# Large attention layers: exponentials behind the next unit's squares and values, reciprocals and probabilities behind its normalisation

## What is computed

```python
q = (hidden_states @ q_proj_w.T).reshape(B, Q, NUM_HEADS, HEAD_DIM).transpose(0, 2, 1, 3)
k = (cross_attention_states @ k_proj_w.T) ...
v = (cross_attention_states @ v_proj_w.T) ...
q = rmsnorm(q, q_norm_w); k = rmsnorm(k, k_norm_w)
scores = jnp.einsum('bhqd,bhkd->bhqk', q, k) * scale + attention_mask
attn = jax.nn.softmax(scores, axis=-1)
out = jnp.einsum('bhqk,bhkd->bhqd', attn, v)
x = x + jnp.tanh(g_xattn[1]) * (out @ o_proj_w.T)
```

## Time and profile before

| | |
|---|---|
| median of 3 runs | 3029.27 us (3025.58 to 3031.83) |
| the profiled execution | 3028.03 us |
| its span, first to last instruction | 3026.2 us |
| TensorE busy | 2552.8 us (84%) |
| VectorE busy | 1838.3 us (61%) |
| ScalarE busy | 1314.6 us (43%) |
| GpSimd busy | 1287.3 us (43%) |
| mean granted TensorE clock | 0.938 of full |

### The profile page before, as it was taken

One profiled execution on the slowest core, in us unless ns is written; L12 is line 12 of the kernel. 1 busy time (PEld: TensorE's weight loads), 2 busy tenths in 40 slices (PEclk: granted clock), 3 DMA queues, 4 the chain that ended last, 5 costly groups with the idle time before them and its releaser, 6 DMA issues. The chain is left out here.

```text
span 3026.2 us, 42470 instructions
## 1 busy us (share of the span) xinstructions
PE 2552.8 (84%) x13827; PEld 2149.3 (71%) x13827; DVE 1838.3 (61%) x3455; ACT 1314.6 (43%) x3752; POOL 1287.3 (43%) x1423
## 2 busy tenths in 40 slices
PE   3899999997679999998878886978579999999655
PEld 2788888875568888887757775745468888888544
DVE  3676777766556666666646664522456666666655
ACT  2454444443235555554424443123145555555223
POOL 4444444442124444444326554333334444444235
PEclk9899999998889999999999997989799999999868
DMA  3101111110002222211000001278111111110037
GB/s 105 49 29 36 33 36 36 36 32 25 13 22 83 82 88 91 77 36 53 32 9 10 8 8 55 56 242 291 47 31 45 32 32 36 33 35 5 9 125 262
DMA packets 69103, 178.95 MB, mean 59 GB/s; under 512 B 10516, under 2 KB 11218, under 8 KB 66683
## 3 DMA queue, kind: packets, MB, share of 16 engines
q1 hardware_dynamic: 52048, 112.25, 11.5%
q0 software_dynamic: 13632, 61.10, 6.1%
q10 hardware_dynamic: 3210, 2.89, 0.3%
HBM read 157.84 MB, written 37.25 MB: 64 GB/s over the span
## 5 line engine op out<-in xcount | busy, mean ns | idle before, releaser
L1991 POOL TENSOR_TENSOR W<-W,rden 128x512 f32<-128x512 f32 x192 | 199.9, 1041 | 839.3 <-DVE rden L1460 839.3
L1167 ACT ACTIVATE W<-S,nmx 128x128 f32<-128x128 f32 x768 | 299.3, 391 | 514.4 <-DVE nmx L1455 514.4
L1952 POOL TENSOR_TENSOR S<-S,mask 128x512 f32<-128x512 f32 x192 | 248.9, 1296 | 107.9 <-ACT S L1011 107.7
L1011 ACT ACTIVATE oT_h<-B_oT 128x512 fp32r<-128x512 f32 x200 | 119.9, 600 | 286.1 <-PE B_oT L733 281.3
L1460 DVE RECIPROCAL rden<-den 128x4 f32<-128x4 f32 x192 | 34.2, 178 | 327.2 <-ACT W L1167 327.2
L1473 DVE SCALAR_TENSOR_TENSOR X<-B_out,gates,X 128x512 f32<-128x512 f32 x216 | 161.5, 747 | 111.3 <-PE B_out L662 111.0
L662 PE MATMUL B_out<-ring_h,oT_h 128*128 128x512 f32 x516 | 208.9, 405 | 18.1 <-DVE X L1473 8.8
L662 PE MATMUL B_qkv<-ring_h,xnT_h 128*128 128x512 f32 x512 | 217.3, 424 | 5.0 <-DVE xnT_l L1309 5.0
L713 PE MATMUL B_s<-kT,qT_h 128*128 128x256 f32 x768 | 207.9, 348 | 4.1 <-DVE S L1452 2.5
L703 PE MATMUL B_qT<-ident,qk 128*128 128x128 f32 x768 | 130.1, 294 | 94.8 <-DVE qk L1423 68.4
L662 PE MATMUL B_out<-ring_l,oT_h 128*128 128x512 f32 x516 | 207.7, 402 | 0.0
(11 more groups left out here) (446 smaller groups left out, 8044.7 us busy)
## 6 DMA issues: line engine op xcount, KB each, us to landing
raw<-in_pieces SPq DMA_DIRECT2D x270, 256.0 KB, 2.7
slots_y<-S SPq DMA_DIRECT2D x31, 256.0 KB, 4.2
slots_y<-y SPq DMA_DIRECT2D x15, 256.0 KB, 5.5
X<-in_x ACTq DMA_DIRECT2D x8, 256.0 KB, 2.8
raw<-in_ctxT SPq DMA_DIRECT2D x8, 256.0 KB, 2.7
rows_x<-xn SPq DMA_DIRECT2D x8, 256.0 KB, 2.0
out_x<-X SPq DMA_DIRECT2D x8, 256.0 KB, 3.6
raw<-in_quant SPq DMA_DIRECT2D x4, 256.0 KB, 2.6
```

The costliest lines, as they stand in the source:

```text
L1011: return act.activation(dst, src, ACT.Copy, scale=scale)
L1167: t = act.activation(W[:, k, cols(r)], S[:, k, cols(r)], ACT.Exp, bias=nmx[:, k, r:r + 1], accum_out=den[:, k, r:r + 1])
L1952: pool.tensor_tensor(S3, S3, m.unsqueeze(1).to_broadcast([P, R, P]), ALU.add).then_inc(*masked.now((layer, u)))
L1991: pool.tensor_tensor(W3, W3, rden[:, k, :].unsqueeze(2).to_broadcast([P, R, P]), ALU.mult).then_inc(*probs.now((layer, u)))
```

## The change

Two order numbers of `Schedule.attention` change. The exponentials of unit i stay in step i + 2 but go from order 60 to 71, behind `project` of unit i + 2. The event `probs` (VectorE's reciprocal and GpSimd's multiplication) goes from step i + 2, order 65, to step i + 3, order 11, behind `normalise` of unit i + 2 and ahead of `times_v`, `turn_p`, `scores`, and of the `mask` of unit i + 1. The instructions themselves, their number and their semaphores are the same, and so are the programs of TensorE and of the SP queue. The `next` events at 90 (and, outside the middle units, at 5) now come ahead of `probs`.

```diff
@@ -141,8 +141,8 @@
             self.at(i + 2, 40, "scores", layer, u)
             self.at(i + 2, 41, "low_scores", layer, u)
             self.at(i + 2, 56, "mask", layer, u)
-            self.at(i + 2, 60, "exp", layer, u)
-            self.at(i + 2, 65, "probs", layer, u)
+            self.at(i + 2, 71, "exp", layer, u)
+            self.at(i + 3, 11, "probs", layer, u)
             self.at(i + lag - 2, 30, "turn_p", layer, u)
             self.at(i + lag - 1, 20, "times_v", layer, u)
             self.at(i + lag, 0, "attn_out", layer, u, needs=five[3:5],
```

## The result

The changed kernel takes 2917.7 us in the median of four runs (2910.31 to 2920.50), against 3029.31 us (3025.58 to 3031.83) before: a ratio of 0.9629, 95% interval 0.9608 to 0.9650, some 112 us less. Its profiled execution was the fastest of the four: 2910.31 us, span 2908.5 us, mean granted clock 0.940 (0.938 before). The spans differ by 3026.2 - 2908.5 = 117.7 us.

The account below looks back on a forecast made before the run. TensorE, the busiest engine, waits for q and k because exponentials precede the square on ScalarE. From 3028.0 us, minus 68 (steady units) and 23 (looser stretches) gives 2937, plus 1.2 for the median: 2938 us, range 2916 to 2984.

Parts of the forecast that it names:

- layer 0's steady gain: Layer 0's middle 48 units: floor 9.50 us, excess 3.0 us per eight-unit cycle, six cycles, 18 us gained.
- the loss of layer 1's first four units: Where layer 1 begins: exponentials leave idle ScalarE time and delay the low-rank copies, 1 us each, minus 4 us.
- Layer 0's two ends and layer 3's end: Two or three units each with a late maximum, 1.4 to 2 us a unit: 12 us gained, an estimate.
- the floor of layers 1 and 3: TensorE's own period in steady units there, taken as 9.64 us from four consecutive transposes without a wait.
- my 50 us: Steady gain of layers 1 and 3: 25 us each, from 4.2 us excess per cycle, six cycles.
- the looser stretches: Units outside the flat stretches: 23 us gained in sum, bounds 42 us above and minus 10 below.
- layer 3's start: Late maximum, exponentials hold square and VectorE's sums: 1.8 us a step, five steps, 9 us gained.
- Layer 1's end: Squares begin long after the projection's end: three units, 2 us each, 6 us gained.
- The first: Rival: probabilities delay the mask addition and eat the cover; half the steady gain and edges, 2984 us; chance 0.2.
- The second: Rival: VectorE or GpSimd held the normalisation anyway, so the time stays at 3029 us; chance 0.03.
- The third: Rival: maximum over 1 us later than summed, each microsecond more costs one per unit; say 3090 us; chance 0.05.
- My cover: Slack of the maximum before the next exponentials are due: about 1 us, in layer 0 0.3 to 0.6 us.

Follow-up runs that it names:

- the half kernel: Against the changed kernel, two of each unit's four exponentials back at order 60, ahead of project, the other two at 71: 2977.3 us, ratio 0.9836.
- the last experiment: Against the changed kernel, the exponentials of layer 1's first four units alone back at order 60: 2917.7 us, ratio 0.9633.
- the kernel with the longer probabilities: Against the changed kernel, one more GpSimd instruction of 128 x 512, adding zero to W, behind each unit's probabilities: 2942.5 us, ratio 0.9709.

## Why the prediction was right, and where it was off

The forecast was 2938 us in a range of 2916 to 2984; 2917.7 us lies in it, near its lower end. The sum said 91 us, the medians gave 112 us and the profiled execution 117.7 us.

Right in mechanism and size: the square within 0.1 us of the projection (0.04); the transposes freed of their wait in all steady units; layer 0's steady gain (17.5 for 18 us); the loss of layer 1's first four units (5.7 for 4, of which the exponentials' place makes 3.3, by the run that puts it back). Layer 0's two ends and layer 3's end gave 13.5 us for 12, but that sum is partly luck: 6.4, 5.5 and 1.6 us for 4 each.

Mis-sized: the floor of layers 1 and 3. I took 9.64 us from four transposes without an idle time in front. It is 9.54 us: (1125.51 - 1049.22) / 8 in the changed kernel.

```profile
1049.22 0.61 PE L703 MATMUL B_qT<-ident,qk 128*128 128x128 f32 x4
...
1125.51 0.62 PE L703 MATMUL B_qT<-ident,qk 128*128 128x128 f32 x4
```

In those units of the kernel before the transposes still followed the normalisation: v_l at +1.20 and transposes at +4.66 us after the projection, the pair that the half kernel shows too (+1.20, +4.67), against +0.94 and +4.57 when nothing stands in front. So they waited some 0.1 us, with no bracket to say so. That is 96 x 0.1 = 10 us of the 12 us by which layers 1 and 3 exceed my 50 us (62.0). Layer 0 could have told: a unit has the same 56 matmuls there, and its floor was 9.50 us.

The windows give the whole of this hidden wait, 21.5 us of busy time over the three layers. The records themselves hardly changed: their lengths, added up over the same matmuls, fall by 4.3 us only (2709.9 to 2705.6). The other 17.2 us is overlap of neighbouring records (1315.4 to 1332.7 us), nearly all of it in front of the transposes: where TensorE waits for less than the tail of the record before, the wait shows as a shorter overlap and not as an idle time. The Trainium skill (Perfetto Trace Analysis, Tensor Engine Instruction (MATMUL, LD_WEIGHTS)) says that the end of a matmul in a trace is an estimate from the instruction's size, not an observation; the lengths that hardly move agree with it.

Mis-sized in the looser stretches: layer 3's start gave 14.6 us for 9. The five steps I had counted gave 7.2 us (74.4 to 67.2). Most of the rest, 5.9 us, is one step that I hadn't seen, 16.98 us long before and 11.10 us after, at the first unit of the second head group (the two other kernels with all exponentials at 60 took 15.7 us there, so 1.2 us of it may be of that one execution). In the kernel before:

```profile
2246.91 0.40 ACT L1167 ACTIVATE W<-S,nmx 128x128 f32<-128x128 f32 x1 [2.67 <-DVE nmx L1455]
...
2248.47 0.61 ACT L1011 ACTIVATE ring_lent_h<-raw 128x512 fp32r<-128x512 f32 x1
...
2248.85 1.04 POOL L1991 TENSOR_TENSOR W<-W,rden 128x512 f32<-128x512 f32 x1 [4.70 <-DVE rden L1460]
2249.84 1.26 POOL L1923 TENSOR_TENSOR ring_lent_l<-raw,ring_lent_h 128x512 fp32r<-128x512 f32 x1
...
2251.20 0.55 PE L662 MATMUL B_qkv<-ring_lent_h,ctxT_h 128*128 128x256 f32 x1 [5.03 <-issue]
```

The copy of the last weight piece stood behind the exponentials, its low part behind the probabilities, and the projection began 0.1 us after the low part ended, after 5.03 us of idle time. In the changed kernel:

```profile
2164.28 0.63 ACT L1011 ACTIVATE ring_lent_h<-raw 128x512 fp32r<-128x512 f32 x1 [0.72 <-DMA raw<-in_pieces]
...
2164.98 1.27 POOL L1923 TENSOR_TENSOR ring_lent_l<-raw,ring_lent_h 128x512 fp32r<-128x512 f32 x1 [1.09 <-ACT ring_lent_h L1011]
...
2166.35 0.36 PE L662 MATMUL B_qkv<-ring_lent_h,ctxT_h 128*128 128x256 f32 x1 [1.36 <-issue]
```

The copy waits for its DMA only, and the projection for 1.36 us. I had listed the weight splits among the work that the moves pass, but only as a delay of the probabilities, never as work that the exponentials hold up.

A term that the sum had at nothing is TensorE's clock. In the step just shown, behind the 5.03 us of idle time, the next matmuls of 128x256 take 0.41 us each at a granted clock of 0.50 (1.2 GHz); behind 1.36 us they take 0.28 us at 1.00 (2.4 GHz). Over the stretches TensorE's own busy time moved with it: layer 0's first eight units from 77.9 to 74.1 us (granted clock 0.86 to 0.91), layer 3's first eight from 78.9 to 75.1 (0.84 to 0.88), layer 1's second four from 49.0 to 44.2 (0.91 to 1.00), and the other way layer 1's first four, from 61.8 to 64.6 (0.81 to 0.79). Net that is 9.6 us of gain beside the idle time (a small part may be overlap of records, as above), which a sum of waits alone can't hold.

Not forecast: the 10.0 us of layer 1's second four units. Of these 4.2 lie in the first period (21.4 to 17.2 us), the one that the last experiment took back, and 5.2 in the last two (14.0 to 9.6 and 10.2 to 9.5 us), where before the maximum came 1.5 and 1.8 us after the projection, as at layer 3's start. Nor did I forecast the 6.7 us in layer 2 and its feed-forward parts, of which about 6 us is no effect of the change: layer 2, from its first to its last transpose (L763), took 239.5 us in the profiled execution before and 233.6 us in this one, but 236.2 to 236.7 us in all the others, the one with both moves taken back in effect (exponentials at 60, probabilities at 42) and the second execution of the changed kernel among them. Layer 1's end gave 3.4 us for 6, since in its two longest steps (14.2 us each) the maximum ends 4.0 us after the projection, and VectorE's v_l and sums stand behind it in either kernel. Between layers 0 and 1 it lost 2.0 us, where the exponentials' move alone gained 5.0: the loss goes with the second move, by a path that no run isolates. The 2.5 us behind layer 3 are within what two executions of the changed kernel differ by there (6.3 us).

The rivals. The first, the probabilities eating the cover, is refuted at the steady period, which is the floor in all eight units, though its mechanism is real: it is what costs 50 us in the kernel with the second move alone. The second falls with the result. The third said that each microsecond beyond the cover costs a microsecond a unit; the kernel with the longer probabilities puts the maximum up to 1.1 us beyond the cover in layer 0 and loses 1.7 us in 48 units; further than that no run goes. My cover was right in layer 0 (0.3 to 0.6 us; 0.41 us measured) and high in layer 1 (about 1 us; the heaviest units have 0.55 us), but the first microsecond past it was cheap: v_h and the square no longer stand behind the exponentials, and only v_l comes later (1.2 instead of 0.35 us behind the projection at most).

## What to carry to other kernels

In an engine's in-order queue, put the instruction that releases the next stage ahead of one whose result is needed a step later, even if the second one's input has been ready for longer. A move into idle time must be checked against each instruction that it now precedes: the probabilities ahead of the mask addition cost 50 us with the gate in place, nothing in the steady part without it, and behind the addition the whole kernel was 8 to 11 us faster still. And don't take an engine's own period from neighbours without an idle bracket alone (9.64 us here) nor from its busy time (463.6 / 48 = 9.66 us a unit before): compare with another stretch that runs the same instructions, as layer 0 with its 9.50 us did. Where a wait goes, look at the granted clock too: behind the long idle times here it was lower, and so the work behind them longer.

## What the runs showed of the hardware

Unexpected was how much waiting of TensorE counts as busy time, 0.15 us a unit over 144 units (21.5 us), four fifths of it as overlap of records that got lost. Then the price of work side by side: with the probabilities of GpSimd beside VectorE's splits, the 119 ring_l went from a mean of 1149 to 1258 ns, and with the probabilities behind the mask addition to 1230 ns, while the mask additions went from 1296 to 1311 and 1255 ns. The Trainium skill (SBUF — State Buffer, Who interferes with whom) lets a VectorE instruction with two SBUF inputs and a GpSimd one that reads SBUF exclude each other for a whole instruction, and the changed kernel's trace agrees with it split by split. Of its 104 ring_l of 128x512, the 14 that meet no GpSimd instruction of over 0.2 us take 0.68 to 0.69 us; of the 89 that start inside one, 81 end 0.54 to 0.58 us behind that instruction's end, however long it still runs, and take up to 1.78 us. The longer means cost nothing in the steady units, where TensorE is idle for 0.5 us in all.
